# Causal zeroes set by DVE in SBUF instead of mask products on PE, with a new order of DVE and Pool work

## What is computed

```python
x = L0_attn_x                                  # (16, 512, 128)
# first block: 16 heads of 8, rotary, causal
q, k, v = heads of layernorm(x) @ wq.T, wk.T, wv.T;  q, k = rope(q), rope(k)
scores = q @ k.T / sqrt(8);  scores = where(key > query, -big, scores)
x = x + (softmax(scores) @ v) @ wo.T
# second block, twice: 8 heads of 64, windows of 64 with the one before
h = shift_token(x); q, k, v = split(h @ wqkv)
q, k = rotary_xpos(l2norm(q) * qs, l2norm(k) * ksc)
x = x + local_attention(q, k, v) @ wo
h = layernorm(shift_token(x)) @ w1 + b1;  x = x + (a * gelu(g)) @ w2 + b2
```

## Time and profile before

| | us |
|---|---|
| median of three runs | 2443.89 (2443.87 to 2459.32) |
| the profiled execution | 2439.99 |
| its span, first to last instruction | 2438.2 |
| PE, DVE, ACT, Pool busy in the span | 2153.6, 1763.4, 1553.0, 1773.9 |

### The profile page before, as it was taken

How to read it: one execution, slowest core, us unless ns; L and a number is a source line. 1 busy time by engine, 2 the same in 40 slices (tenths; PEclk the granted TensorE clock), 3 DMA queues, 4 the chain that set the end, 5 groups by cost and what they waited for, 6 DMA issues and landing times.

```text
span 2438.2 us, 55022 instructions
## 1 busy us (share of the span) xinstructions
PE 2153.6 (88%) x20736; PEld 1447.8 (59%) x20736; DVE 1763.4 (72%) x4632; ACT 1553.0 (64%) x2510; POOL 1773.9 (73%) x1615
## 2 busy tenths in 40 slices
PE   4887899899999989998999999999899999988886
PEld 1444566665666666665666656666566666665654
DVE  4766777787777877788777777778777777666653
ACT  1445666676676667666766766766676667765553
POOL 2126768787777868787686777878787778788882
PEclk9999999999999999999999999999999999999997
DMA  4222121121212111121112112121121211111110
GB/s 138 65 66 54 40 53 49 44 59 45 57 37 60 52 46 49 48 59 46 49 49 59 44 45 58 33 64 51 39 51 47 60 48 36 25 32 27 28 25 23
DMA packets 115081, 119.56 MB, mean 49 GB/s; under 512 B 31945, under 2 KB 88054, under 8 KB 114818
## 3 DMA queue, kind: packets, MB, share of 16 engines
q1 hardware_dynamic: 114818, 116.04, 18.2%
HBM read 55.96 MB, written 20.97 MB: 32 GB/s over the span
## 4 chain that ended last, share of the span: by engine, by line
PE 38%; DVE 21%; ACT 14%; POOL 13%; issue 11%; DMA 1%; SPq 1%; ACTq 0%; DVEq 0%; POOLq 0%
PE ps L734 4%; PE ps L645 4%; POOL inv L1408 4%; DVE ps L977 4%; PE ps L554 4%; PE ps L828 3%; DVE nm L1019 3%; PE ps L587 3%; DVE ss L1029 3%; PE ps L712 3%; PE ps L600 2%; PE ps L567 2%; ACT PT L1190 2%; PE ps L810 2%; PE ps L819 2%
## 5 line engine op out<-in xcount | busy, mean ns | idle before, releaser
L977 DVE CUSTOM_DVE_ANT_0 ps<-ps,causal 128x512 f32<-128x512 f32 (+3 forms) x1024 | 492.4, 506 | 328.3 <-PE ps L587 322.3
L1408 POOL TENSOR_TENSOR inv<-ss,nhalf 128x16 f32<-128x16 f32 x128 | 377.7, 2950 | 394.0 <-DVE QN L1012 394.0
L1190 ACT ACTIVATE PT<-ps 128x512 f32<-128x512 f32 (+1 forms) x768 | 409.1, 536 | 352.5 <-PE ps L602 349.8
L587 PE MATMUL ps<-KA,QA 72*128 72x512 bf16 (+3 forms) x1024 | 275.1, 311 | 77.1 <-DVE nmax L977 72.9
L1397 POOL TENSOR_TENSOR RS<-RAW,rot 128x512 f32<-128x512 f32 x256 | 319.9, 1271 | 0.0
L1403 POOL TENSOR_TENSOR RC<-RC,RS 128x1024 f32<-128x1024 f32 x128 | 300.9, 2351 | 18.4
L600 PE MATMUL ps<-QA,KA 75*128 75x512 bf16 (+3 forms) x1024 | 286.8, 306 | 27.8 <-ACT PT L1190 26.0
L1386 POOL TENSOR_TENSOR RC<-RAW,rot 128x1024 f32<-128x1024 f32 x128 | 307.9, 2405 | 0.0
L1019 DVE TENSOR_REDUCE nm<-ps 128x8 f32<-128x1024 f32 x128 | 156.4, 1222 | 119.3 <-PE ps L734 119.3
L699 PE MATMUL ps<-wqkv,ZT 128*128 128x512 f32 x512 | 241.9, 595 | 0.0
L587 PEld LDWEIGHTS ps<-KA,QA 72*128 72x128 bf16 x1024 | 96.4, 100 | 235.3 <-DVE nmax L977 142.4
(11 more groups left out here) (122 smaller groups left out, 5304.9 us busy)
## 6 DMA issues: line engine op xcount, KB each, us to landing
V_even<-V_odd SPq DMA_DIRECT2D x256, 130.0 KB, 2.6
QA<-parts SPq DMA_DIRECT2D x192, 96.0 KB
KA<-parts SPq DMA_DIRECT2D x192, 96.0 KB
parts<-qkp SPq DMA_DIRECT2D x32, 384.0 KB, 3.5
X_next<-in_x SPq DMA_DIRECT2D x16, 256.0 KB, 3.1
X<-in_x SPq DMA_DIRECT2D x16, 256.0 KB, 2.9
x_kept<-X SPq DMA_DIRECT2D x16, 256.0 KB, 3.8
XR<-x_kept SPq DMA_DIRECT2D x32, 128.0 KB, 2.9
```

The source lines that it names most:

```text
L587: last = pe.matmul(dst[:, c0:c0 + w], QA[e][0:QK_ROWS, h % UNIT, qt * P:(qt + 1) * P], KA[e][0:QK_ROWS, h % UNIT, 0:w], start=True, stop=True)
L977: ins = v.tensor_tensor_reduce(for_max(i, x)[:, c0:c0 + w], for_max(i, x)[:, c0:c0 + w], causal[:, S - w:S], -1.0, -NEG, ALU.add, ALU.min, ...
L1190: a.activation(PT1[:, h % UNIT, c0:c0 + w], for_exp(i, x)[:, 0:w], ACT.Exp, scale=SCALE1).then_inc(exped.sem, 1)
L1408: g.tensor_tensor(inv[:, :], ss[:, :], nhalf[:, :], ALU.pow).then_inc(inv_ready.sem, 1)
```

## The change

- Line 602 goes: PE makes no product with `causal_t`. The exponentials above the diagonal are then taken of unmasked scores.
- `causal_t` becomes f32, 0 above the diagonal and 3e38 elsewhere, and DVE takes in SBUF the minimum of it and each diagonal block of `PT1` (`cut_ahead`): once a slot, four `tensor_tensor` of 128x2x128 for two heads. It waits for all exponentials of the slot, stands behind step 5 and ahead of `gate_up` of the third chunk and the `next_*` work there; `values` waits for `cut` in place of `exped`. This is done in 128 slots, the first 19 of them ahead of the first tile of the second block.
- DVE's order: `unit_heads` moves from behind step 0 to behind step 1 and `add_heads`; `norms` (and `shifted_tokens`) move behind `gate_up` and `heads_over_sum`; `next_cos` of the second weight moves to the head of its slot; the sum of the rotary products (line 949) becomes `next_sum` and moves to the end of the slot, behind the cuts; `next_low` stands behind step 2.
- Three small `tensor_scalar` of DVE become `tensor_tensor` with a constant tile (`eps`, `tiny`); line 1032 is one of them. Pool sets the two tiles at the start.
- Pool's `first_normalise` of lane 0 moves from slot 7 to slot 8, and SP's `load_first` of lane 1, which waits for it, from slot 8 to slot 10.

```diff
@@ PE, scores_exp
-                        pe.matmul(dst[:, c0:c0 + w], KA[e][0:ROWS, h % UNIT, kt * P:(kt + 1) * P],
-                                  QA[e][0:ROWS, h % UNIT, kt * P:S], start=True, stop=False)
-                        last = pe.matmul(dst[:, c0:c0 + P], identb[:, :], causal_t[:, :],
-                                         start=False, stop=True)
+                        last = pe.matmul(dst[:, c0:c0 + w], KA[e][0:ROWS, h % UNIT, kt * P:(kt + 1) * P],
+                                         QA[e][0:ROWS, h % UNIT, kt * P:S], start=True, stop=True)
@@ PE, values
-                    pe.wait_ge(*past(exped.sem, exped.at(i, PARTS1 * UNIT * (u + 1))))
+                    pe.wait_ge(*past(cut.sem, cut.at(i, 2 * (u + 1))))
@@ DVE
+                def cut_ahead(s):
+                    pair = STEPS * s // 2 + (AHEAD - BEHIND) // 2
+                    v.wait_ge(*past(exped.sem, exped.at(i, PARTS1 * (2 * pair + 2))))
+                    n = 2 * pair % UNIT
+                    for kt in range(NT):
+                        c0 = SEG[kt][0]
+                        block = PT1[:, n:n + 2, c0:c0 + P]
+                        ins = v.tensor_tensor(block, block, causal_t[:, :].unsqueeze(1).to_broadcast([P, 2, P]), ALU.min)
+                    ins.then_inc(cut.sem, 1)
...
-                    v.tensor_scalar(ss[:, :], ss[:, :], 1e-24, None, ALU.max).then_inc(ss_ready.sem, 1)
+                    v.tensor_tensor(ss[:, :], ss[:, :], tiny[:, :], ALU.max).then_inc(ss_ready.sem, 1)
...
+                    if s % 8 == 4 and lives(i, 2):
+                        next_cos(two, z, 1)
                     if tile_in(i, s):
                         maxima(s)
                     attention_step(s, 0)
+                    attention_step(s, 1)
+                    if tile_in(i, s - 1):
+                        add_heads(s - 1)
                     if tile_in(i, s + 1):
                         unit_heads(s + 1)
+                    attention_step(s, 2)
...
                     attention_step(s, 3)
-                    if tile_in(i, s + 3):
-                        norms(s + 3)
-                    if tile_in(i, s - 1):
-                        shifted_tokens(s - 1)
                     if b:
                         gate_up(p, 0)
                         gate_up(p, 1)
                     if s % 2 and unit_in(i, (s + 17) // 2):
                         heads_over_sum((s + 17) // 2)
+                    if tile_in(i, s + 3):
+                        norms(s + 3)
+                    if tile_in(i, s - 1):
+                        shifted_tokens(s - 1)
...
                     attention_step(s, 5)
+                    if head_in(i, STEPS * s + AHEAD - BEHIND):
+                        cut_ahead(s)
                     if a:
                         gate_up(p, 2)
                     if s % 8 == 0 and lives(i, 2):
                         next_moments(two, z)
                     if s % 8 == 2 and lives(i, 2):
                         next_sin(two, z, 0)
+                        next_sum(two, z, 0)
+                    if s % 8 == 4 and lives(i, 2):
+                        next_sum(two, z, 1)
@@ Pool
-                    if s == 7 and lives(i, 1):
+                    if s == 8 and lives(i, 1):
                         first_normalise(later(i, 1), 0)
```

More of the change, by code:

```diff
@@ L188, in build @@
         causal = sb("causal", [P, S], BF16)
-        causal_t = sb("causal_t", [P, P], BF16)
+        causal_t = sb("causal_t", [P, P])
         band = sb("band", [P, 2, P], BF16)
@@ L202, in build @@
         nhalf = sb("nhalf", [P, 2 * H2])
+        tiny = sb("tiny", [P, 2 * H2])
+        eps = sb("eps", [P, NT])
         spare = sb("spare", [P, 1])
@@ L323, in build @@
         exped = count("exped", PARTS1 * H1 * LANES)
+        cut = count("cut", 2 * UNITS)
         pv_done = count("pv_done", UNITS)
@@ L388, in build @@
         N_FIRST, N_CONST = 4, 10 + L * 7
-        N_MADE = LANES + 9
+        N_MADE = 2 * LANES + 9
         def past(sem, value):
@@ L518, in body @@
                             keep_first(1, z)
-                    if s == 8 and lives(i, 1):
+                    if s == 10 and lives(i, 1):
                         sp.wait_ge(*past(ln_out.sem[0], ln_out.at(later(i, 1), 1)))
@@ L930, in moments @@
                 v.wait_ge(*past(meant.sem[z], meant.at(k, 1)))
-                v.tensor_scalar(veps[:, :], mv[:, :, 1], EPS, None, ALU.add).then_inc(done.sem[z], 1)
+                v.tensor_tensor(veps[:, :], mv[:, :, 1], eps[:, :], ALU.add).then_inc(done.sem[z], 1)
             def next_moments(n, z):
@@ L947, in next_sin, with next_sum @@
                 v.tensor_tensor(rope_s[:, :], a_ps, sin1[:, :], ALU.mult).then_inc(roped.sem[z], 1)
+            def next_sum(n, z, w):
                 v.wait_ge(*past(roped.sem[z], roped.at(n, 2 * w + 2)))
@@ L1065, in tile_moments @@
                     v.wait_ge(*past(tile_mean.sem, tile_mean.at(i, m + 1)))
-                    v.tensor_scalar(veps[z][:, tt:tt + 1], mv[z][:, tt, 1:2], EPS, None,
+                    v.tensor_tensor(veps[z][:, tt:tt + 1], mv[z][:, tt, 1:2], eps[:, 0:1],
                                     ALU.add).then_inc(tile_var.sem, 1)
@@ L1100, in body @@
                     attention_step(s, 0)
+                    attention_step(s, 1)
+                    if tile_in(i, s - 1):
+                        add_heads(s - 1)
                     if tile_in(i, s + 1):
                         unit_heads(s + 1)
+                    attention_step(s, 2)
                     if s % 8 == 4 and lives(i, 2):
-                        next_cos(two, z, 1)
                         next_low(two, z, 0)
@@ L1107, in body @@
                         next_low(two, z, 1)
-                    attention_step(s, 1)
-                    if tile_in(i, s - 1):
-                        add_heads(s - 1)
-                    attention_step(s, 2)
                     if s % 8 == 3 and lives(i, 2):
@@ L1336, in _ @@
             g.memset(nhalf[:, :], -0.5).then_inc(made, 1)
+            g.memset(tiny[:, :], 1e-24).then_inc(made, 1)
+            g.memset(eps[:, :], EPS).then_inc(made, 1)
             g.wait_ge(made, N_MADE)
@@ L1455, in constants @@
         "ident": np.eye(P, dtype=f), "identb": np.eye(P, dtype=bf),
-        "causal": np.concatenate([np.zeros((P, S - P)), np.where(k > q, f(NEG), f(0))], 1).astype(bf), "causal_t": np.where(q > k, f(NEG), f(0)).astype(bf),
+        "causal": np.concatenate([np.zeros((P, S - P)), np.where(k > q, f(NEG), f(0))], 1).astype(bf), "causal_t": np.where(q > k, f(0), f(-NEG)).astype(f),
         "band": np.where(np.stack(rows, 1), f(0), f(NEG)).astype(bf),
```

## The result

| | us |
|---|---|
| before, median of 4 runs | 2447.55 (2443.87 to 2459.32) |
| after, median of 4 runs | 2722.47 (2720.12 to 2729.42) |
| ratio, with its 95% interval | 1.1116 (1.1078 to 1.1154) |
| after, the profiled execution, and its span | 2729.42, 2727.6 |

The change makes the kernel 11% slower. The forecast was 4.7%, with a range that ended at 2645 us. The sign was right, and more than half of the size was missing.

A forecast was written before the change was run, and what follows sets the result against it. PE and DVE bound the kernel in turn at slot boundaries. A body: 18.4 + 12.1 - 2.4 - 8.8 - 2.0 = +17.3 us, +118 over 6.8 bodies; with ends +12 and -16, +114, forecast 2558 us, range 2380 to 2645.

The forecast's parts named there:

- The order: DVE's and Pool's new instruction order: fewer waits for maxima and G gain 8.8 us a body, later `first_normalise` 2.
- cover of `values`: Even-slot boundary: the 2.3 us of `values` hides most work queued behind the cuts, costed at nothing; uncovered, 0.7 to 2 us.
- Waits for maxima and G: PE's waits for DVE: half of 11.9 us for maxima and 2.8 for G go, 8.8 us a body.
- `first_normalise`: Pool's layer norm a slot later frees Pool for the maxima's parts in slot 8: gain of 2 us a body.
- The ends: First 19 slots with cuts cost 12 us (0 to 28); the last 347 us gain 16 (0 to 27).
- The cuts at the boundaries: Cuts delay line 1019 in odd slots by 10.4 us a body and `values` in even slots by 8.0.
- The meetings with Pool: Cuts on DVE wait for Pool's instructions, 0.76 us a slot in the mean: +12.1 us a body.
- Rival 1: Cuts alternate with Pool, a slot losing some 1.7 us: 2660 us; chance 0.17 for 2610 to 2700.
- Rival 2: Cuts on DVE don't meet Pool, 82 us less: 2476 us; chance 0.16 for 2415 to 2510.
- Rival 3: Slot boundary has room, cuts run before line 734 ends, a quarter of 18.4 us left: 2370 us; chance 0.24.
- The masks: Mask products leaving PE gain 2.4 us a body, bounds 0 and 7.7.
- rival 4: PE's mask time comes back in full, 7.7 us a body: 2522 us; chance 0.43 together with the forecast.

The follow-up runs named there:

- e1: Kernel before with DVE's cuts in place of PE's mask products, everything else in the old order: 2603.48 us, 1.0686.
- e2: New order of DVE and Pool with the mask products still on PE and no cuts, against the kernel before: 2500.80 us, 1.0257.
- e4: Kernel after with QN alone put back behind step 0: 2573.09 us, 1.0561 of the kernel before.
- e6: New order with masks on PE and no cuts, but QN put back in its old place: 2438.66 us, 0.9999 of the kernel before.
- e7: Kernel after with each cut replaced by an equally long one-input tensor_reduce, setting no causal zeroes: 2657.29 us, 1.0906 of the kernel before.
- e9: Kernel after without the clamp of ss (line 1046): 2711.62 us, 1.1132 of the kernel before.
- e3: Kernel before without the mask products and without cuts, so no causal zeroes are set: 2428.74 us, 0.9962.
- e11: New order with QN in its old place, masks on PE, two ss buffers and the clamp on Pool: 2359.25 us, 0.9691 of the kernel before.
- e5: Kernel after with two ss buffers in turn, so norms waits for the inv of the tile before: 2697.90 us, 1.1075 of the kernel before.

## Why the prediction was wrong

A body took 318.9 us in place of 284.2 (forecast 301.5). The 34.8 us between them, by place, from the same starts:

| a body, us | forecast | e1 (cuts alone) | e2 (order alone) | e4 (all, QN early) | after |
|---|---|---|---|---|---|
| into the 8 even slots: step 0's maxima later | 10.4 | 10.0 | 0.0 | 10.5 | 13.7 |
| into the 8 odd slots: end of local scores to the next step 0 | 8.0 | 11.8 | 3.3 | 11.8 | 18.0 |
| inside even slots, step 0's maxima to the end of local scores | | -1.9 | +0.7 | -8.0 | +0.9 |
| odd slots | | -1.5 | +4.4 | +3.5 | +2.2 |
| in no place: meetings +12.1, masks -2.4, order -8.8 and -2.0 | -1.1 | | | | |
| sum | +17.3 | +18.4 | +8.4 | +17.9 | +34.8 |

What PE's lower clock adds is inside these figures and was not taken apart; in the bodies shown the granted clock is 0.97 for 0.99.

**What failed is the step "The order"**, which forecast 8.8 and 2.0 us a body of gain, and 16 at the end. Measured alone it was a loss of 2.6 points, 62 us (e2), and with the cuts one of 4.3 points, some 105 us (e1 to after). Most of it is QN's late place: with QN put back, the order costs nothing (e6), and with the cuts half of the whole loss is gone (e4). The prediction had seen that QN's late place moves Pool's chain; it used this only to place Pool's sum against the cuts, and gave the path back to DVE no price. The same shift puts inv in front of `norms`, RC under the clamp, and both in front of step 4. In even slots QN came 7.0 us into the slot for 3.1, `norms` at 11.4 for 8.9, step 4 at 15.1 for 12.8; 1.7 us of each are step 0's maxima, which the cuts make late. The gain was there to be had: with QN early and the same cuts and order (e4) the stretch inside an even slot is 1.0 us shorter than before (13.7 for 14.7), 8.0 us a body where 8.8 were forecast, and 14.8 with QN late. That e4's body, at +17.9, comes near the forecast's +17.3 is luck in part: the missing cover of `values` stands in for meetings that hardly took place.

**Waits for maxima and G.** G's wait of line 829 did go, in the last stretch too (1.9 us of 27.1). That of line 590 stayed at 11.4 us in the body shown: the waits for step 1's maxima, which had stood behind QN, did go, but were 3.1 us and not half of 11.9; those for step 0's, which are later, behind the cuts, rose from 3.7 to 5.5; those for step 4's stayed (5.0 and 5.1).

**`first_normalise`** was priced at -2.0 us a body. Slot 9 went from 15.2 to 20.1 us in e2, to 21.0 in e6 and to 18.9 in after, as Pool comes to inv late there and `norms` with it (11.2 us into the slot in e2, 7.5 before); the two layer norms of Pool back to back are shown at e6. By this it was a loss of 3.7 us a body in after, some 25 us in all, and in e2 4.9 of the body's 8.4 us; no run moved it alone.

**The ends.** From line 1019 (now 1033) of the first tile without cuts to the end, the last stretch took 298.4 us before, 301.5 in e2 and 307.7 after: it was to lose 16 us and got 9 longer. With QN early it did get shorter, to 286.6 in e6 and 279.6 in e4; but it is 290.8 in e1 too, which has the old order, so not all of that is the order's. The first tile starts 28.7 us later than before, forecast 12, with 28 as the bound.

**The cuts at the boundaries.** Into even slots 10.4 us were forecast and e1 shows 10.0. Into odd slots the cover did not hold: `values` waits for `add_attention` and `next_sin`, and PE's turns wait for what DVE does behind the cuts. The prediction named this, with 0.7 to 2 us in six slots, and took nothing; e1 shows 3.8 us a body more than its 8.0, and after 10.0 more.

**The meetings with Pool.** Forecast 0.76 us a slot. In e1 it is 4 x (439 - 419) = 0.08 us, in after 4 x (503 - 419) = 0.34 us; taking them away there gave some 51 us (e7), not 82. Rival 1, by which Pool would get its turn between two cuts, is out: the median of a cut stays at 414 ns in after, and in e9's slot the last three cuts fit in the 1.28 us behind the sum's end. Rival 2, cuts clear of Pool, is nearly what e1 is. e1's 165 us are 44 over the forecast's cuts and masks without the meetings, (18.4 - 2.4) x 6.8 + 12 = 121: the two largest pieces are the missing cover of `values`, 3.8 x 6.8 = 26, and the head, 22, where line 1019 of the first tile starts 34 us later than before; smaller ones go both ways. Rival 3, by which the cuts would come earlier than line 734's end by over 1 us, did not come either: in the two places shown the cuts start 0.34 and 0.46 us ahead of line 735's end, where the exponentials ended 0.49 and 0.55 us ahead of line 734's.

**The masks.** 10 us measured in e3 (4 to 15) against 16: right in kind, a little too large; rival 4, all 61 us, is out. **Line 1032 as a `tensor_tensor`**: 1042 ns for 932, and 918 in e4: nothing, right. **Line 1066 as a `tensor_tensor`** has no term in the prediction: it went from 154 ns to 752, which is 0.6 us a slot just ahead of step 4, 77 us of DVE's time in all. What of it is on the path is not known. **The rotary sum**: line 952 at 692 ns in the median, 740 at most, right.

**The range** ended at 2645 since the order's gain was bounded by 0 from below: a loss was given no chance. A moved instruction whose result another engine waits for can lose, and here nothing in the trace excluded it: the earlier trace rows show 53.1 us of Pool's waits for QN.

What stays open: how much of the loss line 1080's new form and `first_normalise`'s new slot make by themselves. Each is read from the traces, and the next runs would be the kernel after, and e11, with the one or the other put back.

## What to carry to other kernels

Before an instruction is moved back in its queue, follow its result through the other engine and back to the queue it stands in: here QN, inv, `norms` and step 4 were one loop, and the 2.5 us by which QN is later in after than in e4 came back as 1.3 at step 4. Where several waits end at the same place, take them all away before judging one, for each alone gave 0 to 2.1 points and together they gave 6.8. A tiny DVE instruction with a long mean duration can be a wait for Pool in disguise, as line 1080's 752 ns were for one element a partition: see whether its end follows one of Pool's. Moving the clamp to Pool was worth 1.6 points here. And an instruction that is given another form with a constant tile as second input can pick up such a wait, as line 1066 did (154 ns in the old form, 752 in the new).

## What the runs showed of the hardware

- A cut (128x256, two SBUF inputs) that started while Pool's sum was under way ended behind it: 74 did so in after, 71 of them the first of their four, and all 74 ended 0.28 to 0.35 us behind the sum. They took 0.42 to 2.58 us, where the median of the 512 is 0.41. The others of the four then ran at their own pace (e9's slot: 2.61 us for four, 1.28 of them after the sum's end; in the slot shown of after, where the first cut started only 0.09 us ahead of the sum's end, four took 1.43). With one input, 165 reductions of the same elements started beside the same sum and took 0.41 to 0.42 us (e7).
- The same was seen for 16 elements: 0.17 us of work took up to 3.44 us, and 127 of 128 ended 0.03 to 0.04 us behind Pool's RC or RS (line 1046 in after). The second input was not what decided there: line 1032 before, a `tensor_scalar` with `ss` as its one input from SBUF, took 0.18 to 3.46 us, and 126 of 128 ended 0.03 to 0.04 us behind RC or RS.
- One element is enough: line 1066 as a `tensor_scalar` took 153 to 156 ns at all 128 places, 126 of which began while Pool's RC, RS or sum was under way; as a `tensor_tensor` with two SBUF inputs (line 1080) it took 752 ns in the mean and 2.32 us at most, and 125 of 128 ended 0.01 to 0.02 us behind one of Pool's.
- Not every Pool instruction with inputs in SBUF was seen to hold DVE up: beside Pool's power DVE instructions of 128x512 with two SBUF inputs (lines 956 and 960) took their own 0.68 to 0.69 us, all 48 times in after, and the clamp of 128x16 took 0.17 to 0.18 us, all 22 times in e5.
- Pool's power on 128x16 takes 2.92 us, ten times its clamp of the same shape (0.30 us).
